# A fused decoder layer on one core: the gate's sigmoid and bias sum made by GpSimd, and the loop's items in another order on the five engines

## What is computed

```python
x = x + attn(layernorm(x)); x = x + xattn(layernorm(x), ctx); x = x + ffn(layernorm(x))
# in ffn, the gate:
scores = sigmoid(xt @ gate.T)                      # 8 numbers per token
_, sel = top_k(scores + expert_bias, 2)
routed = xt[token] * scores_of_sel                 # then silu(xb @ w1.T) * (xb @ w3.T) @ w2.T
```

## Time and profile before

| what | us |
|---|---|
| time, median of 3 runs | 1011.39 (1009.79 to 1011.78) |
| time of the profiled execution | 1009.28 |
| span of its profile | 1007.5 |
| busy: DVE / POOL / ACT / PE | 910.5 / 748.0 / 733.1 / 722.3 |

### The profile page before, as it was taken

How to read it: one execution, slowest core, us unless ns; L and a number is a source line. 1 busy time by engine, 2 the same in 40 slices (tenths; PEclk the granted TensorE clock), 3 DMA queues, 4 the chain that set the end, 5 groups by cost and what they waited for, 6 DMA issues and landing times.

```text
span 1007.5 us, 21210 instructions
## 1 busy us (share of the span) xinstructions
PE 722.3 (72%) x7072; PEld 398.6 (40%) x7072; DVE 910.5 (90%) x1841; ACT 733.1 (73%) x989; POOL 748.0 (74%) x728
## 2 busy tenths in 40 slices
PE   6965766777677768687777777686868777777674
PEld 4543222344343434343444434343434444343243
DVE  3896967999999999999999999999999999999942
ACT  2633756878877888787777778788878878787842
POOL 6689988979797979797897979797979889710000
PEclk9986786989997989888888979798988889797955
DMA  6011795999899999999998999999999989999971
GB/s 238 1 43 47 131 168 105 173 153 184 169 183 172 157 174 159 167 173 172 166 173 161 180 157 192 170 158 174 169 158 172 175 163 169 158 195 163 192 147 31
DMA packets 574018, 156.01 MB, mean 155 GB/s; under 512 B 567251, under 2 KB 571862, under 8 KB 573526
## 3 DMA queue, kind: packets, MB, share of 16 engines
q1 hardware_dynamic: 573910, 154.67, 86.7%
HBM read 9.93 MB, written 2.10 MB: 12 GB/s over the span
## 4 chain that ended last, share of the span: by engine, by line
DVE 45%; issue 24%; PE 19%; ACT 4%; DMA 2%; SPq 2%; POOL 2%; DVEq 0%; POOLq 0%; ACTq 0%
DVE score L1134 30%; PE ps_score L1458 7%; PE ps L1316 6%; DVE gate L1168 3%; ACT prob L824 2%; PE ps_score L1316 2%; SPq L423 2%; DVE exp_bias L1144 2%; DVE early L1184 2%; DMA prob_t<-prob 2%; ACT queries L806 1%; DVE gate L1166 1%; DVE q_parts L1117 1%; PE ps_pv L1488 1%; PE ps L1437 1%
## 5 line engine op out<-in xcount | busy, mean ns | idle before, releaser
L1134 DVE TENSOR_SCALAR_CACHE_REDUCE score<-ps_score,q_neg 128x1024 f32<-128x1024 f32 x512 | 636.2, 1278 | 17.0 <-PE ps_score L1458 15.5
L824 ACT ACTIVATE prob<-score,exp_bias 128x2048 uint16<-128x2048 f32 x256 | 511.1, 1997 | 11.6 <-DVE exp_bias L1144 9.3
L1458 PE MATMUL ps_score<-keys,queries 128*128 128x512 bf16 x1024 | 351.8, 444 | 195.0 <-DVE score L1134 156.3
L1458 PEld LDWEIGHTS ps_score<-keys,queries 128*128 128x128 bf16 x1024 | 75.4, 104 | 370.7 <-DVE score L1134 306.0
L527 POOL TENSOR_TENSOR product<-hs_exp,v_tok 128x1024 f32<-128x1024 f32 x64 | 148.5, 2342 | 18.0 <-ACT hs_exp L789 17.9
L534 POOL TENSOR_TENSOR product<-product 128x512 f32<-128x512 f32 x128 | 158.9, 1263 | 0.0
L527 POOL TENSOR_TENSOR product<-qk_rot 128x1024 f32<-128x1024 f32 x64 | 149.6, 2350 | 0.3 <-POOL qk_rot L520 0.2
L545 POOL TENSOR_TENSOR product<-product 128x512 f32<-128x512 f32 x64 | 82.4, 1288 | 5.9 <-POOL product L534 5.9
L877 ACT ACTIVATE routed_both<-normed,routed_gate 128x256 bf16<-128x256 f32 x128 | 57.1, 496 | 37.8 <-DVE routed_gate L1179 37.8
L1488 PE MATMUL ps_pv<-prob_t,values 128*32 128x128 f16 x4096 | 73.0, 227 | 11.0 <-DMA prob_t<-prob 10.9
L1488 PEld LDWEIGHTS ps_pv<-prob_t,values 128*32 128x32 f16 x4096 | 62.0, 101 | 40.4 <-issue 40.4
(11 more groups left out here) (124 smaller groups left out, 1125.8 us busy)
## 6 DMA issues: line engine op xcount, KB each, us to landing
prob_t<-prob SPq DMA_TRANSPOSE x256, 4.7
prob_t<-in_w SPq DMA_DIRECT2D x3, 1024.0 KB, 4.8
x_in<-in_x SPq DMA_DIRECT2D x16, 128.0 KB, 3.1
score<-in_cond_t SPq DMA_DIRECT2D x4, 512.0 KB, 6.6
out<-x_out SPq DMA_DIRECT2D x16, 128.0 KB, 2.5
w_qkv<-in_w_qkv SPq DMA_DIRECT2D x1, 768.0 KB, 4.3
early<-in_w_kv SPq DMA_DIRECT2D x1, 512.0 KB
w_s<-in_w_s SPq DMA_DIRECT2D x3, 128.0 KB
```

Of the source, the lines that this page charges most:

```text
L824: act.activation(prob[:, s, :].bitcast(U16), score[:, s, :], ACT.Exp, bias=exp_bias[:, s:s + 1], scale=-1.0, accum_out=prob_sum[:, t.par, ...
L1134: dve.tensor_scalar(score[:, s, HALF * i:HALF * i + HALF], ps_score[:, score_slot(t.count(H, h), i)].rearrange("p b k -> p (b k)"), q_neg[ ...
L1458: mm = pe.matmul(ps_score[:, score_slot(n, i), b, :], queries[:, t.par, h // 2, h % 2, :], keys[:, h // 2, k0:k0 + KEYS], start=True, stop ...
```

## The change

GpSimd gets an item `gate_sums(m)` that makes the sigmoid (a tensor_scalar) and adds the bias (a tensor_tensor) and signals them on `gate_chain`, as DVE did; DVE's `choose` keeps the other steps and waits for the second signal. POOL's item stands behind `ln_scale(1)` and just ahead of `score_products(3)`. And on all five engines the loop's items are put in another order. The moves that the text comes to, as engine: item, h before -> h after ("early" is ahead of the head's own item, "late" behind it):

- DVE: `choose` 10 late -> 11 late; `cross_sum` 4 -> 1; `cross_norm` 5 -> 4; `ln_gather(2)` 6 -> 5; `largest_query` 14 early -> 12 late; `quantise_queries` 14 late -> 13 early; `largest_score` 14 late -> 13 late; `expert_hidden` 1 late and 3 early -> 2 early and 2 late; `shared_hidden` 14 late -> 15 early.
- ACT: `gate_tanhs` 8 -> 9; `route` 10 to 13 -> 11 to 12; `head_exp` stays at 14, early; `hidden_tanh` 0 -> 1.
- PE: `ln_turn(2)` and `gate_and_shared(0)` 10 -> 11; `sum_turn` 6 -> 5, beside `queries_or_keys(1)`; `experts_out` 3 -> 4, early; `q_turn` 15 -> 13.
- SP: the load of tile t + 3 at h = 14 instead of 11; `turn_routed` at 11 instead of 12.
- POOL: `fold_8(0)` goes from behind `score_products(3)` to ahead of it, and some foldings are interleaved.

The preparation ahead of the loop is untouched. The diff, with the loops of ACT, DVE and PE cut:

```diff
@@ -434,13 +434,13 @@
 
             def body(t):
                 for h in range(H):
-                    if (t + -2).exists() and h == 13:
-                        store(t + -2)
-                    if (t + 3).exists() and h == 11:
+                    if (t + 3).exists() and h == 14:
                         load_x(t + 3)
                     if t.exists() and by_dma(h):
                         turn(h, t)
-                    if (t + -1).exists() and h == 12:
+                    if (t + -2).exists() and h == 12:
+                        store(t + -2)
+                    if (t + -1).exists() and h == 11:
                         turn_routed(t + -1)
 
             load_x(Tile(2))
@@ -490,6 +490,19 @@
                     pool.sem_inc(settled, 1)
                 pool.tensor_tensor(ho_n[:], ho[:], over(hs_inv[:], HD), ALU.mult).then_inc(ho_done, 1)
 
+            def gate_sums(t):
+
+                sig, biased = gate[:, 0, :], gate[:, 1, :]
+                pool.wait_ge(gate_tanhed, t.count(1, 1))
+                pool.sem_inc(settled, 1)
+                if (due := t.due(6)) is not None:
+                    pool.wait_ge(gate_chain, due)
+                    pool.sem_inc(settled, 1)
+                pool.tensor_scalar(sig, gate_tanh[:], 0.5, 0.5, ALU.mult, ALU.add).then_inc(gate_chain, 1)
+                pool.wait_ge(gate_chain, t.count(6, 1))
+                pool.sem_inc(settled, 1)
+                pool.tensor_tensor(biased, sig, b_expert[:], ALU.add).then_inc(gate_chain, 1)
+
             def spread_sums(t):
 
                 pool.wait_ge(sum_inverted, t.count(1, 1))
@@ -589,43 +602,48 @@
 
             def body(t):
                 a, n, m = t + 2, t + 1, t + -1
+                if n.exists():
+                    value_products(2, n)
                 if a.exists() and not t.starts():
                     ln_scale(0, a)
                 if n.exists():
-                    value_products(2, n)
                     value_products(3, n)
                     fold_one(6, n)
                     fold_one(7, n)
-                    fold_8(3, n)
                 if m.exists():
                     spread_sums(m)
                 if n.exists():
+                    fold_8(3, n)
                     fold_4(3, n)
-                    fold_2(3, n)
                 if a.exists():
                     rope(a)
                 if n.exists():
+                    fold_2(3, n)
+                if a.exists():
+                    score_products(0, a)
+                if n.exists():
                     norm_ho(n)
                 if a.exists():
-                    score_products(0, a)
+                    score_products(1, a)
                 if m.exists():
                     ln_scale(2, m)
                 if a.exists():
-                    score_products(1, a)
-                    score_products(2, a)
                     fold_one(0, a)
                     fold_one(1, a)
-                    score_products(3, a)
+                    score_products(2, a)
+                    fold_8(0, a)
                 if n.exists():
                     ln_scale(1, n)
+                if m.exists():
+                    gate_sums(m)
                 if a.exists():
-                    fold_8(0, a)
-                    fold_4(0, a)
+                    score_products(3, a)
                     fold_one(2, a)
                     fold_one(3, a)
-                    fold_2(0, a)
+                    fold_4(0, a)
                     fold_8(1, a)
                     fold_4(1, a)
+                    fold_2(0, a)
                     fold_2(1, a)
                     shift_scores(a)
                     value_products(0, a)
@@ -889,61 +907,62 @@
...
                 for h in range(H):
-                    if a.exists() and h == 14:
-                        head_exp(a)
...
+                    if o.exists() and h == 1:
+                        hidden_tanh(0, o)
+                    if m.exists() and h == 12:
+                        route(2, m)
+                    if m.exists() and h == 5:
+                        keep_two(m)
+                    if n.exists() and h == 11 + late:
+                        ln_apply(1, n)
+                    if m.exists() and h == 12:
+                        route(3, m)
+                    if a.exists() and h == 5:
+                        keep_qkv(1, a)
+                    if m.exists() and h == 8:
+                        ln_apply(2, m)
...
+                    if m.exists() and h == 9:
+                        ln_keep(2, m)
...
+                    if m.exists() and h == 12:
+                        route(4, m)
+                    if m.exists() and h == 11:
+                        route(0, m)
+                    if m.exists() and h == 12:
+                        route(5, m)
+                    if a.exists() and h == 14:
+                        head_exp(a)
+                    if m.exists() and h == 13:
+                        shared_tanhs(m)
+                    if o.exists() and h == 1:
+                        hidden_tanh(1, o)
...
+                    if m.exists() and h == 12:
+                        route(6, m)
+                        route(7, m)
+                    if n.exists() and h == 11 + late:
+                        ln_keep(1, n)
                     if n.exists() and h == min(H - 1, 14 + late):
...
-                    if m.exists() and h == 10:
-                        route(0, m)
...
-                        ln_apply(2, m)
-                        ln_keep(2, m)
                     if t.exists():
                         exp_head(h, t)
+                    if m.exists() and h == 9:
+                        gate_tanhs(m)
+                    if a.exists() and h == 1 + behind:
+                        ln_apply(0, a)
+                        ln_keep(0, a)
+                    if m.exists() and h == 11:
+                        route(1, m)
...
-                    if m.exists() and h == 8:
-                        gate_tanhs(m)
...
@@ -1162,11 +1181,6 @@
             def choose(t):
 
                 sig, biased, marked, best = (gate[:, i, :] for i in range(4))
-                dve.wait_ge(gate_tanhed, t.count(1, 1))
-                dve.tensor_scalar(sig, gate_tanh[:], 0.5, 0.5, ALU.mult, ALU.add).then_inc(gate_chain, 1)
-                dve.wait_ge(gate_chain, t.count(6, 1))
-                dve.scalar_tensor_tensor(out=biased, in0=sig, scalar=1.0, in1=b_expert[:], op0=ALU.mult, op1=ALU.add
-                                         ).then_inc(gate_chain, 1)
                 dve.wait_ge(gate_chain, t.count(6, 2))
                 dve.max(best, biased).then_inc(gate_chain, 1)
                 dve.wait_ge(gate_chain, t.count(6, 3))
@@ -1220,55 +1234,55 @@
...
+                    if n.exists() and h == 10 + late:
+                        ln_combine(1, n)
+                    if o.exists() and h == 2:
+                        expert_hidden(0, o)
...
-                    if n.exists() and h == min(H - 1, 14 + late):
-                        largest_query(n)
+                    if n.exists() and h == 13 + late:
+                        quantise_queries(n)
+                    if m.exists() and h == 15:
+                        shared_hidden(m)
                     if t.exists():
                         keep_scores(h, t)
-                    if t.starts() and h == 4:
...
-                    if a.exists() and h == 14:
-                        largest_score(a)
...
-                    if m.exists() and h == (4 if t.exists() else 2):
-                        cross_sum(m)
+                        ln_combine(2, m)
+                    if a.exists() and h == 0:
+                        loaded(a)
+                        ln_gather(0, x_in[:, a.par, :], a)
                     if n.exists() and h == 9 + late:
...
+                    if m.exists() and h == 4:
+                        cross_norm(m)
...
+                    if m.exists() and h == 11:
+                        choose(m)
...
+                    if o.exists() and h == 2:
+                        expert_hidden(1, o)
+                    if m.exists() and h == (1 if t.exists() else 0):
+                        cross_sum(m)
...
+                    if n.exists() and h == 12 + late:
+                        largest_query(n)
+                    if m.exists() and h == 5:
+                        dve.wait_ge(xo_projected, m.count(1, 1))
+                        ln_gather(2, bank[6][:, 0:D], m)
+                    if a.exists() and h == 13:
+                        largest_score(a)
...
-                    if m.exists() and h == 10:
-                        choose(m)
-                    if n.exists() and h == min(H - 1, 14 + late):
-                        quantise_queries(n)
...
-                    if m.exists() and h == 5:
-                        cross_norm(m)
                     if t.exists():
                         bias(h, t)
@@ -1567,65 +1581,66 @@
...
-                    if n.exists() and h == 13 + late:
```

(43 more changed lines are left out.)

117 lines of the change are left out of this document (25 added, 92 removed).

## The result

The changed kernel takes 1003.57 us (median of 4 runs, 1001.72 to 1005.91) where the kernel before takes 1011.41 (1009.79 to 1011.78): a ratio of 0.9927, 95% interval 0.9903 to 0.995. It is faster by 7.8 us, half of the 15.1 forecast, and within the range of 977 to 1013. The profiled execution took 1001.72 us with a span of 999.8.

The account below looks back on a forecast made before the run. DVE was taken to set the pace at 54.6 us a tile, then a 53.4 us cycle through POOL and DVE: 1.2 us in 13 tiles, 15.6, less 0.5 at the ends, 15.1 off 1011.4, giving 996.3; range 977 to 1013.

Parts of the forecast that it names:

- DVE bounds the kernel before: In the loop before the change DVE sets the pace, busy for 53.5 of 54.6 us in one tile.
- Steps 1 to 5: One round from POOL's bias sum to the next tile's: 2.3 + 7.5 + 3.2 + 10.05 + 30.35 = 53.4 us.
- L1179 stays exposed: Last step of `choose` on DVE still waits out POOL's product; sum to next bias takes 2.3 us, not 0.7.
- No slack, no price: Load of x behind head 13's transpose: lands 16.6 us after `choose`, when DVE asks for it, so nothing was charged.
- step 2: From the end of `choose` on DVE to the row maxima (`largest_score`): 7.5 us.
- slower rival: Load of x lands late and DVE waits 2.8 us a tile; 1022 us, deciding from 2.0 us of wait; chance 0.14.
- 53.4 cycle: The new round through POOL's bias sum, `choose`, row maxima and POOL's body, 53.4 us, longer than DVE's 52.6.
- About 0.3 until the query projection is there: Last term between the end of `choose` and the row maxima: DVE's wait for the query projection, about 0.3 us.
- 54.6 - 53.4: Old tile period less the new cycle: 1.2 us gained in each of 13 tiles, 15.6 in all.
- The ends: First tile of the loop unchanged; the very last gate, wholly exposed, costs 0.5 us more.
- The full gain at DVE: Rival: the cycle falls below DVE's floor of 52.6 us, or towards 51.1; time 975 to 986; chance 0.28.
- The lock that only moves: Rival: POOL's folding holds L1179, cycle 54.6, no gain, 1011; chance 0.16, shared with several small waits eating the gain.

Follow-up runs that it names:

- e4: The kernel before, in its own order, with only the move of the two gate operations to POOL (`gate_sums` between `fold_one(1)` and `score_products(3)`): 1007.11 us.
- e3: The changed kernel with the last operation of `choose` (mask and product with the sigmoid) replaced by a MAX8 of the sigmoids: 988.46 us.
- e1: The changed kernel with the load of x for tile t + 3 put back from h = 14 to h = 11: 998.91 us.
- e8: The changed kernel with the load of x at h = 11 and ACT's `ln_keep(1)` ahead of `route(0)`: 991.35 us.
- e9: e8 with POOL's `score_products(3)` put ahead of the gate's sums and `ln_scale(1)` behind them: 991.87 us.
- e11: e8 with ACT's `head_exp` put ahead of head 13's exponential instead of behind it: 992.13 us.
- e2: The changed kernel with two POOL items exchanged, `gate_sums` ahead of `ln_scale(1)`: 1003.34 us.

## Why the prediction was right in its cycle and wrong in its size

The forecast was 15.1 us and the measured gain 7.8. The loop was to give 15.6 and gave 4.7; the ends were to cost 0.5 and gave 3.0. So part of the half that arrived is luck.

- *DVE bounds the kernel before, and two of its operations are held by POOL.* Right for the kernel before, where DVE stood idle for about 1 us a tile. e4 adds that this alone decides nothing: take the work off DVE without new order and the time turns into wait and hold.
- *Steps 1 to 5.* Right to 0.2 us each, and 53.45 against 53.4 in sum. The sums on POOL cost 0.20 + 0.18 + 0.20 = 0.58, against 0.65. That L1179 stays exposed was right, and worth 12 us (e3).
- *"No slack, no price"* is the step that failed. I had put the load's arrival and DVE's demand on the same 16.6 us after `choose`, and took that for free. In the ten tiles of the loop in which DVE waited, the load was issued at 14.1 on average and landed at 17.2 (16.5 to 17.9), and DVE asked for it at 16.4 (16.2 to 16.6). It was late in every one, by 0.26 to 1.51 us, 8.8 in all. In the other two tiles DVE was itself over 1 us late, by step 2. Putting the load back took 3.4 us off in e1. The slower rival named this very mechanism, but put its threshold at 2.0 us of wait. The room was 0.3 to 0.6: beyond it DVE's wait delays POOL's `rope` by way of PE and ACT and so falls into the 53.4 cycle.
- *"About 0.3 until the query projection is there"* was mis-sized. It was about 0.2 in quiet tiles and some 1.5 more in two, because `ln_keep(1)` stands behind `route(0)`, the new order let the held L1193 block both, and in those two tiles PE's granted clock had fallen to 0.50 by the time its operand came. I had followed that queue for DVE and POOL, but not for ACT. With the load in time it was worth 7.7 us (e1 to e8).
- *"54.6 - 53.4"* had its first term too large. 54.6 was the period of the tile I read; the mean over the thirteen was 54.41, so about 2.5 of the 15.6 us were never there. The other 8.3 of the 10.9 that are missing in the loop are the mean period of 54.04 against 53.4.
- With both undone (e8) the loop gains 14.8 us from the second to the fifteenth tile, against a forecast of 15.6, at a period of 53.26: the five steps were the right model of the kernel, without its disturbances.
- *The ends.* I gave +0.5. The stretch from the fifteenth tile's first head to the end took 136.5 us instead of 139.0, so the changed kernel gained 2.5 there and 0.5 ahead of the loop; I have no experiment on why. The span was 7.7 us shorter, and these 3.0 are a good third of it.
- *The rivals.* The full gain at DVE didn't come, and e9 and e11 show that it wasn't near: below 53.3 another round waits at about 53. The lock that only moves is what e4 does alone; with the order it is half true, as the hold moved to L1193 but the cycle is still shorter.
- *The signs.* L1193 took 0.97 to 1.92 us in the twelve cycles, mostly near 1.7, and the idle time of over 1 us ahead of bn_stats, named as the sign of a price wrongly put at nothing, did come, in four tiles. Two signs failed: POOL waited 2.2 us a tile for the row maxima where less than 1 was said, though the prediction's own 9.8 against 8 us of foldings gives 1.8; and MAX8 waited for POOL in a few tiles only (0.31 to 1.00 us), as DVE mostly came with the sum or up to 0.8 us behind it.

## What to carry to other kernels

When two engines' streams are bound into one cycle, write the cycle down as steps, but give each "arrives just in time" a price: here both times were estimates, they were off by 0.6 and 0.2 us, and the load came late in ten of twelve tiles. Then follow that wait through all the queues, not only the one in which it stands. Take the period to be beaten as a mean over the loop, not from one tile. When an operation is held by another engine's instruction, moving it frees nothing by itself; look for what its next neighbour will be held by, and for items that queue behind its consumer without needing it, such as `ln_keep(1)` behind `route(0)`. Here undoing two such moves gave 11 us, more than the change itself.

## What the runs showed of the hardware

- A held 128x8 operation ends with POOL's instruction, so its cost is set by when that ends and not by its own size: in the tiles shown it took 1.70 us in the changed kernel and 1.84 in e2, over the twelve cycles 0.97 to 1.92, and MAX8 had means of 0.166 to 0.170 in all kernels and took no more in the middle of a product.
- POOL's own 128x8 operations took 0.196 (tensor_scalar) and 0.203 us (tensor_tensor), where the same work free of holds took 0.14 to 0.17 on DVE.
- One idle stretch of 2.39 us, for which ACT's order was to blame, ended with PE at a granted clock of 0.50 from 738 on, and the matmuls behind it took 2.07 us in place of 1.13. A late operand was paid for twice. Two waits of 2.14 us in the same place ended one at 0.50 and one still at 1.00, so the length of such a wait does not tell whether it is paid twice.
